# KDA stage: another order of masks, scores and convolutions, and the query's norm taken out of the scores

## The chip, the cores and the metric

One core of a Trainium2 chip runs the whole program in one launch. The metric is device time in microseconds (us), lower is better. Engines: PE does the matmuls, ACT the activations, DVE and POOL the elementwise work, SP starts the transfers.

## What is computed

A network of eight sub-layers runs over 8 sequences of 256 tokens and 256 channels, each as x + layer(layernorm(x)): rwkv7, ffn, rglru, ffn, kda, moe, gqa, moe. The change is in kda, a delta rule with a decay per channel, 16 heads of 128 channels:

```
q, k, v = silu(conv4(x @ Wq)), silu(conv4(x @ Wk)), silu(conv4(x @ Wv))
q, k    = q * rsqrt(sum(q*q) + 1e-6) * 128**-0.5,  k * rsqrt(sum(k*k) + 1e-6)
decay   = exp(-exp(A_log) * softplus(x @ Wfa @ Wfb + dt_bias))
beta    = sigmoid(x @ Wb)
S_t     = decay_t * S_(t-1), then S_t += beta_t * k_t (v_t - k_t S_t);   o_t = q_t S_t
out     = (o * rsqrt(mean(o*o) + 1e-6) * norm_w * sigmoid(x @ Wga @ Wgb)) @ Wo
```

o is linear in q. So a factor on q comes out of o, and the output norm divides it out again, except in its epsilon.

## The kernel before

All activations stay in SBUF. In the KDA stage a *pass* is one head with half of the batch (4 sequences, `UNITS`), 16 heads x 2 halves = 32 passes, written out one after the other without a barrier between them. In a pass each engine runs a fixed list of calls, and its order is the order in the code: `chain_pe`, `chain_act`, `chain_dve`, `chain_pool`. Engines meet through counting semaphores only; an engine that comes to a wait stands, and all that is behind it stands too.

A pass mixes the work of three heads or halves:

- *the chain* of the current one: seven levels l (blocks of 1, 2, 4 ... 64 tokens). POOL scales the query rows and the columns and widens the decays (L1975, L2006, L1983, L1984), DVE scales the key rows (`a_rows`, also L1975), PE makes the scores of a level (`scores`, L2039), DVE masks them into lt and aq_b (`masks`, L2224, L2230). The inverse of a triangular matrix grows level by level: `lt_times_t(l)` on PE (L2064), a copy by ACT (`copy_x(l)`, L2151), `t_times_x(l)` on PE (L2073, L2076), an addition by DVE (`update(l)`, L2245). The last level has forms of its own: `last_scores` (L2051), `last_masks`, `last_x` (L2084), `last_dt` (L2090).
- *the front* of the next one: the decay (low-rank product, clip, exp, log of 1+exp), the convolutions (three taps each on DVE, L1797, over a scaled copy that ACT makes), silu, transposes of the values, and for query and key a square, a sum over channels on PE (`squares`, L1714), logarithm (L1771), exp(-x/2) (`root`, L1785) and a scaling on DVE (`q_row`, `a_row`). `decays` (L1790) makes the decay factors that POOL's first rows wait for. `ahead.project` are the query and key projections (L1681) for the pass after, whose results ACT copies out of PSUM (L1721, L1722).
- *the tail* of the one before: output gate (sigmoid), the state, y, its square sum, `log` (L1934) and `root` (L1939), scaling, the output product `out(k)` (L1911) and the addition to the residual stream on DVE (`residual`, L1968).

Every engine returns to its chain's start when its list ends. PE's list begins with the gate matmuls (L1664, `tail.gate`). PSUM has eight banks: 0 and 1 take the scores and the second head projection, 2 and 3 the products, 4 and 5 the tail, 6 and 7 the front, the first head projection and the second output product `out(1)`. So PE's `out(1)` waits until ACT has copied the first head projection, and the second head projection waits until the last scores are copied:

```python
            pe.wait_ge(n.aq_in_sb, at(n.aq_in_sb, 2))
            ahead.project(1)
            pe.wait_ge(n.ylog, at(n.ylog, 1))
            tail.out(0)
            pe.wait_ge(m.head_read, at(m.head_read, 2))
            tail.out(1)
```

ACT evaluates its functions by tables. Where an activation needs another table than the one that is loaded, the program has an instruction ACT_TABLE_LOAD ahead of it; copies, squares and scalings need none of their own.

Of the kernel before, what the change touches and what calls it, by code (L numbers as in the profile page):

```python
# [17 lines left out]
ALU = mybir.AluOpType  # L18
# [1500 lines left out]
L2_EPS = 1e-6  # L1519
B_LEVELS = LEVELS - 1  # L1520
# [3 lines left out]
def kda(nc, g, a):  # L1524
    with ExitStack() as ctx:
# [6 lines left out]
        with ExitStack() as ctx2:  # L1532
# [28 lines left out]
            with nc.Fori(0, LN_STEPS) as b:  # L1561
                cols = seq_cols(b, LN_COLS // SEQ)
                with nc.Block() as block:
# [16 lines left out]
                    def _(act):  # L1580
# [17 lines left out]
        t1, t2, t3, v_in = (s.sb(x, wide) for x in ("t1", "t2", "t3", "v_in"))  # L1598
        ops = [Names(q=s.sb(f"q{i}", wide), a=s.sb(f"a{i}", wide), f=s.sb(f"f{i}", wide), col=s.sb(f"col{i}", wide),
                     v=s.sb(f"vt{i}", [P, QT, UNITS, P])) for i in range(2)]  # L1600
# [4 lines left out]
        lt6 = s.sb("lt6", [HALF, MATS, HALF])  # L1605
# [4 lines left out]
        bg, e, z = (s.sb(x, [P, UNITS, P]) for x in ("bg", "e", "z"))  # L1610
        d = s.sb("d", [P, QT, UNITS, P])
# [8 lines left out]
                    "dve_step")  # L1620
# [6 lines left out]
            head_ready=2, head_read=4, proj_ready=1, proj_read=2, conv_ready=3, silu_ready=3, sq_ready=2, ss_ready=2,  # L1627
            ss_read=2, rs_ready=2, vt_ready=1, vt_in_sb=1, u_ready=1, log_u=1, inv_ready=1, corr=2, softplus_ready=1,
            decay_ready=1, rows_ready=3, scaled=2 * B_LEVELS, rows_scaled=B_LEVELS, g_step=2 * LEVELS, g_clear=1,
# [47 lines left out]
        def project_pe(w, quad, i, bank, done):  # L1677
            for hf in range(2):
                for k in range(KD):
                    col = K_QKV + (i * KD + k) * P  # L1680
                    last = nc.tensor.matmul(psum(g, bank + hf, BANK), w[:, col:col + P],  # L1681
                                            xn_all[:, k, bass.ds(quad * QUAD + hf * BANK, BANK)], start=k == 0,
                                            stop=k == KD - 1)
            last.then_inc(done, 1)

        def front_pe(pe, o, w, quad):
# [19 lines left out]
            def squares(i):  # L1706
                if i == 0:
                    pe.wait_ge(m.vt_in_sb, at(m.vt_in_sb, 1))
                else:
                    pe.wait_ge(m.ss_read, at(m.ss_read, 1))  # L1710
                pe.wait_ge(m.sq_ready, at(m.sq_ready, i + 1))
                src = (t2, t3)[i]
                for hf in range(2):
                    last = nc.tensor.matmul(psum(g, FRONT + hf, BANK), g.ones_w[:], src[:, 2 * hf:2 * hf + 2],  # L1714
# [5 lines left out]
        def project_act(i, w, bank, done):  # L1720
            nc.scalar.activation(pre[i % 2][:, :, CONV - 1:], two(bank), ACT.Copy).then_inc(done, 1)  # L1721
            nc.scalar.activation(cv[i % 2][:], two(bank), ACT.Identity,  # L1722
                                 scale=w_vec(w, K_CONV + i * CONV + CONV - 1)).then_inc(done, 1)
# [9 lines left out]
        def front_act(act, o, w):  # L1733
# [15 lines left out]
            def silu(i):  # L1749
                if i == 0 and turn.index:  # L1750
                    act.wait_ge(n.final_scaled, at(n.final_scaled, 0))
                act.wait_ge(m.conv_ready, at(m.conv_ready, i + 1))
                nc.scalar.activation((o.q, o.a, v_in)[i][:], cv[i % 2][:], ACT.Silu).then_inc(m.silu_ready, 1)
# [6 lines left out]
            def square(i):  # L1760
                act.wait_ge(m.silu_ready, at(m.silu_ready, i + 1))
                nc.scalar.activation((t2, t3)[i][:], (o.q, o.a)[i][:], ACT.Square).then_inc(m.sq_ready, 1)
# [6 lines left out]
            def log_sum(i):  # L1769
                act.wait_ge(m.ss_ready, at(m.ss_ready, i + 1))  # L1770
                nc.scalar.activation((t2, t3)[i][:], two(FRONT), ACT.Ln, bias=g.eps[:, 2:3]).then_inc(m.ss_read, 1)  # L1771
# [10 lines left out]
            def root(i):  # L1782
                act.wait_ge(m.ss_read, at(m.ss_read, i + 1))
                dst = (t2, t3)[i]
                nc.scalar.activation(dst[:], dst[:], ACT.Exp, scale=-0.5).then_inc(m.rs_ready, 1)  # L1785
# [6 lines left out]
            return Calls(decay=decay, exp_decay=exp_decay, project=project, silu=silu, square=square,  # L1792
# [3 lines left out]
        def tap_dve(step, done, i, j, w):  # L1796
            ins = nc.vector.scalar_tensor_tensor(cv[i % 2][:], pre[i % 2][:, :, j:j + SEQ],  # L1797
                                                 w_vec(w, K_CONV + i * CONV + j), cv[i % 2][:], ALU.mult, ALU.add)
# [5 lines left out]
        def front_dve(dve, step, o, w):  # L1804
# [33 lines left out]
            def a_row():  # L1838
                dve.wait_ge(m.rs_ready, at(m.rs_ready, 2))
# [3 lines left out]
            def column():  # L1843
                dve.wait_ge(m.rows_ready, at(m.rows_ready, 2))
# [4 lines left out]
            return Calls(clip=clip, tap=tap, corr=corr, q_row=q_row, a_row=a_row, column=column)  # L1849

        def tail_pe(pe, o, w, quad):
# [48 lines left out]
            def square_sums():  # L1900
                pe.wait_ge(n.gated, at(n.gated, 2))
                pe.wait_ge(n.ysq, at(n.ysq, 2))
# [15 lines left out]
        def tail_act(act):  # L1918
# [13 lines left out]
            def log():  # L1932
                act.wait_ge(n.yss_ready, at(n.yss_ready, 1))
                nc.scalar.activation(y_sq[:], two(TAIL), ACT.Ln, scale=1.0 / KDA_HEAD, bias=g.eps[:, 2:3]  # L1934
# [8 lines left out]
        def tail_dve(dve, o, w, quad):  # L1943
# [15 lines left out]

            def scale():  # L1960
# [9 lines left out]
            return Calls(inner=inner, right_side=right_side, gate=gate, scale=scale, residual=residual)  # L1970
# [6 lines left out]
        def widen(step, o, l):  # L1977

            h = 1 << l
            blocks = [P, UNITS * SEQ // (2 * h), h]  # L1980
            second_total = halves(o.f[:], h, 1)[:, :, h - 1:h].to_broadcast(blocks)
            first_total = halves(o.f[:], h, 0)[:, :, h - 1:h].to_broadcast(blocks)
            step(nc.gpsimd.tensor_tensor(halves(decay_g[:], h, 0), halves(decay_g[:], h, 0), second_total, ALU.mult))  # L1983
            step(nc.gpsimd.tensor_tensor(halves(o.f[:], h, 1), halves(o.f[:], h, 1), first_total, ALU.mult))  # L1984

        def first_rows(pool, step, o):
# [3 lines left out]
            pool.wait_ge(m.rows_ready, at(m.rows_ready, 2))  # L1990
            for r in range(2):
# [1426 lines left out]
```

## Time and profile before

| | |
|---|---|
| median of 3 runs | 6270.61 us (6264.56 to 6274.58) |
| the profiled execution | 6272.03 us |
| its span | 6270.3 us |
| PE busy, share of the span | 5487.5 us, 88% |
| DVE | 3220.0 us, 51% |
| ACT | 2789.8 us, 44% |
| POOL | 2304.6 us, 37% |
| KDA passes | from about 2171 to 4350 us of the span |

The span is the time on the core between first and last instruction; the execution's time has a few microseconds around it. Busy shares are of the whole program, in which the KDA passes are about a third.

### The profile page before, as it was taken

To read this page: it belongs to the slowest core of one execution; us is meant where nothing else is said; L and a number is where in the kernel's file an instruction comes from. 1 tells how busy PE (TensorE), PEld (TensorE's weight loads), DVE (VectorE), ACT (ScalarE), POOL (GpSimd) and SP (SyncE) were. 2 spreads that over 40 slices of the span, in tenths; PEclk is the share of its full clock that TensorE was granted. 3 is DMA by queue.
4 is the path that set the end of the run, shared out by engine and by line. 5 is a ranking of instruction groups with operands and counts; after the bars stand their busy time and mean duration, and the time that the engine had idled before them with its cause. 6 is when DMAs were issued, how large, how long until landed. Compare 5 with 4: busy or idle time off the path is not lost. (4 is left out here: it accounts for less than half of the span.)

```text
span 6270.3 us, 125078 instructions
## 1 busy us (share of the span) xinstructions
PE 5487.5 (88%) x53008; PEld 3632.2 (58%) x53008; DVE 3220.0 (51%) x4649; ACT 2789.8 (44%) x5107; POOL 2304.6 (37%) x1583
## 2 busy tenths in 40 slices
PE   6888699755999599989989989998999988889999
PEld 5777466543666266666666666665444456664444
DVE  5555444434444376776776677675212166552221
ACT  3233444454444456555655655665211166662111
POOL 4554100001000176777777677675222200002222
PEclk8999799877999799999999999999999988889999
DMA  0000100000000000000000000000211100002111
GB/s 29 3 2 2 33 1 1 16 0 33 1 1 3 22 17 23 18 17 23 18 17 17 24 17 17 23 18 9 107 40 40 34 11 0 0 1 108 39 40 46
DMA packets 60618, 137.02 MB, mean 22 GB/s; under 512 B 11638, under 2 KB 24054, under 8 KB 58842
## 3 DMA queue, kind: packets, MB, share of 16 engines
q1 hardware_dynamic: 60122, 129.79, 6.2%
q8 instruction: 386, 6.32, 0.4%
q14 instruction: 110, 0.90, 0.0%
HBM read 127.26 MB, written 2.50 MB: 21 GB/s over the span
## 5 line engine op out<-in xcount | busy, mean ns | idle before, releaser
L607 PE MATMUL ps<-moe_xn_all,moe_w 128*128 128x512 f32 x1792 | 810.5, 595 | 0.0
L720 DVE TENSOR_TENSOR moe_h<-moe_silu,ps 128x512 f32<-128x512 f32 x224 | 153.9, 687 | 936.2 <-ACT moe_silu L662 929.1
L607 PEld LDWEIGHTS ps<-moe_xn_all,moe_w 128*128 128x128 f32 x1792 | 341.2, 191 | 424.1 <-issue 423.5
L662 ACT ACTIVATE moe_silu<-ps 128x512 f32<-128x512 f32 x224 | 133.8, 597 | 986.5 <-PE ps L607 986.4
L1797 DVE SCALAR_TENSOR_TENSOR kda_cv<-kda_pre,kda_w_front,kda_cv 128x1024 f32<-128x1024 f32 x297 | 554.8, 1885 | 1.3
L563 POOL TENSOR_TENSOR moe_h<-moe_h,moe_cb 128x512 f32<-128x512 f32 x176 | 233.6, 1327 | 696.4 <-DVE moe_h L720 696.4
L1983 POOL TENSOR_TENSOR kda_g<-kda_g,kda_f 128x512 f32<-128x512 f32 x225 | 395.4, 1757 | 205.7 <-DVE kda_rows L1975 197.1
L617 PE MATMUL ps<-moe_h,moe_w 128*128 128x512 f32 x896 | 420.4, 592 | 0.0
L1681 PE MATMUL ps<-kda_xn_all,kda_w_front 128*128 128x512 f32 x808 | 373.6, 606 | 26.0 <-DMA kda_w_front<-in_Kw 23.5
L1975 POOL TENSOR_TENSOR kda_rows<-kda_q,kda_f 128x512 f32<-128x512 f32 x225 | 361.1, 1605 | 16.6 <-POOL kda_f L1984 1.6
L1984 POOL TENSOR_TENSOR kda_f<-kda_f 128x512 f32<-128x512 f32 x225 | 313.9, 1395 | 17.6
L2006 POOL TENSOR_TENSOR kda_cols<-kda_col,kda_g 128x512 f32<-128x512 f32 x192 | 318.6, 1659 | 0.0
L2064 PE MATMUL ps<-kda_t,kda_lt 64*64 64x64 f32 x5120 | 192.3, 227 | 143.4 <-DVE kda_lt L2224 143.4
L2073 PE MATMUL ps<-kda_x_sb,kda_t 64*64 64x32 f32 x5120 | 310.8, 221 | 0.0
L2076 PE MATMUL ps<-kda_t,kda_x_sb 64*64 64x32 f32 x5120 | 307.0, 219 | 0.0
L617 PEld LDWEIGHTS ps<-moe_h,moe_w 128*128 128x128 f32 x896 | 170.2, 190 | 214.3 <-issue 213.3
L2073 PEld LDWEIGHTS ps<-kda_x_sb,kda_t 64*64 64x64 f32 x5120 | 255.6, 135 | 42.2 <-issue 31.8
L2064 PEld LDWEIGHTS ps<-kda_t,kda_lt 64*64 64x64 f32 x5120 | 169.7, 140 | 167.1 <-DVE kda_lt L2224 166.9
L148 POOL TENSOR_TENSOR moe_xn_all<-moe_xn_all,moe_ln_rstd_b 128x1024 f32<-128x1024 f32 x8 | 18.9, 2366 | 665.8 <-DVE moe_ln_rstd_b L240 665.8
L2076 PEld LDWEIGHTS ps<-kda_t,kda_x_sb 64*64 64x64 f32 x5120 | 256.2, 135 | 0.0
L870 ACT ACTIVATE gqa_p<-ps,gqa_nmax 128x256 f32<-128x256 f32 x512 | 236.6, 491 | 36.1 <-DVE gqa_nmax L936 36.1
L1681 PEld LDWEIGHTS ps<-kda_xn_all,kda_w_front 128*128 128x128 f32 x808 | 146.9, 192 | 181.3 <-issue 148.1
(505 smaller groups left out, 12513.3 us busy)
## 6 DMA issues: line engine op xcount, KB each, us to landing
kda_col<-kda_beta SPq DMA_DIRECT2D x34, 512.0 KB, 3.9
moe_w<-in_Mw SPq DMA_DIRECT2D x6, 2816.0 KB, 19.6
moe_cb<-kda_beta SPq DMA_DIRECT2D x64, 256.0 KB, 3.1
kda_w_front<-in_Kw SPq DMA_DIRECT2D x34, 455.0 KB, 4.7
moe_cb<-kda_beta SPq DMA_DIRECT2D x32, 224.0 KB, 2.9
kda_w_out<-in_Kw SPq DMA_DIRECT2D x32, 192.5 KB, 2.4
moe_cb<-kda_beta SPq DMA_DIRECT2D x32, 192.0 KB, 2.8
moe_cb<-kda_beta SPq DMA_DIRECT2D x32, 160.0 KB, 2.7
```

The costliest lines, as they stand in the source:

```text
L607: last = nc.tensor.matmul(ps_gu[u % 2][r], w13[:, k, i, r], n.xn[:, k, cols(c)], start=k == 0, stop=k == KD - 1)
L617: last = nc.tensor.matmul(ps_y[d], w2[:, i, d * P:(d + 1) * P], h[:, u % H_BUFS], start=i == 0, stop=i == M_TILES - 1)
L870: last = nc.scalar.activation(n.p[:, i % 3, j, 0:w], src, ACT.Exp, scale=n.scale, bias=n.nmax[:, i % 2, j:j + 1], accum_out=n.sums[:, q, s ...
L1681: last = nc.tensor.matmul(psum(g, bank + hf, BANK), w[:, col:col + P], xn_all[:, k, bass.ds(quad * QUAD + hf * BANK, BANK)], start=k == 0, ...
L1797: ins = nc.vector.scalar_tensor_tensor(cv[i % 2][:], pre[i % 2][:, :, j:j + SEQ], w_vec(w, K_CONV + i * CONV + j), cv[i % 2][:], ALU.mult, ...
L1975: engine.tensor_tensor(out, halves((o.a, o.q)[r][:], h, 1), halves(o.f[:], h, 1), ALU.mult).then_inc(done, 1)
L1983: step(nc.gpsimd.tensor_tensor(halves(decay_g[:], h, 0), halves(decay_g[:], h, 0), second_total, ALU.mult))
L1984: step(nc.gpsimd.tensor_tensor(halves(o.f[:], h, 1), halves(o.f[:], h, 1), first_total, ALU.mult))
L2006: nc.gpsimd.tensor_tensor(halves(cols_s[l % 2][:], h, 0), halves(cur.col[:], h, 0), halves(decay_g[:], h, 0), ALU.mult).then_inc(n.scaled, 1)
L2064: last = nc.tensor.matmul(ps_x[b, mt], lt[b, l, mt], rhs, start=True, stop=True)
L2073: nc.tensor.matmul(ps_dt[b, mt, 0], t[b, mt, 1], own_half(x_sb[b, mt], h, 0), start=True, stop=True)
L2076: last = nc.tensor.matmul(ps_dt[b, mt, 1], x_sb[b, mt], own_half(t[b, mt, 1], h, 1), start=True, stop=True)
```

## The change

1. The query is no longer scaled. Its square is kept (`q_square`, a new buffer q_sq for each half), and `with_query` on DVE adds 128 x 1e-6 x 128 times that square to the square of y before the sum over channels. The output norm's epsilon becomes 128e-6 x 1e-6. On PE one square sum goes, on ACT one logarithm and one root, on DVE `q_row`.
2. The convolutions are done value, key, query (`PART`). The head projections that are made ahead are now value and key, and the query's silu comes late in the pass.
3. PE's order: scores(l+1) stand behind lt_times_t(l) and ahead of t_times_x(l), the two head projections ahead of last_x and last_dt.
4. DVE: masks stand ahead of clip, taps and updates. POOL: the columns are widened without waiting for the key rows, and the first query rows are scaled behind the widening of the columns.
5. ACT's list in a new order, below.
6. lt6 shares the memory of z; a mask table that nothing reads is no longer loaded.

The core of the diff (taps, signatures and the same edits in the prologue are left out):

```diff
+        PART = (2, 1, 0)
...
             def values():
                 pe.wait_ge(m.proj_read, at(m.proj_read, 2))
-                pe.wait_ge(m.silu_ready, at(m.silu_ready, 3))
+                pe.wait_ge(m.silu_ready, at(m.silu_ready, 1))
...
+            def q_square():
+                act.wait_ge(m.silu_ready, at(m.silu_ready, 3))
+                if turn.index:
+                    act.wait_ge(m.ysum_ready, at(m.ysum_ready, 1))
+                nc.scalar.activation(o.q_sq[:], o.q[:], ACT.Square).then_inc(m.qsq_ready, 1)
...
-            def q_row():
-                dve.wait_ge(m.rs_ready, at(m.rs_ready, 1))
-                nc.vector.scalar_tensor_tensor(o.q[:], o.q[:], float(KDA_HEAD) ** -0.5, t2[:], ALU.mult,
-                                               ALU.mult).then_inc(m.rows_ready, 1)
...
+            def with_query():
+                dve.wait_ge(n.ysq, at(n.ysq, 2))
+                if turn.index:
+                    dve.wait_ge(m.qsq_ready, at(m.qsq_ready, -1))
+                nc.vector.scalar_tensor_tensor(y_sq[:], o.q_sq[:], QUERY_EPS * KDA_HEAD, y_sq[:], ALU.mult,
+                                               ALU.add).then_inc(m.ysum_ready, 1)
...
@@ chain_act, behind tail.gate and f.decay @@
-            f.exp_decay()
             tail.state()
             copy_x(1)
+            f.exp_decay()
+            tail.square(0)
+            copy_x(2)
             f.silu(0)
-            tail.square(0)
             f.project()
-            copy_x(2)
-            f.square(0)
+            copy_x(3)
+            f.values()
+            tail.square(1)
+            copy_x(4)
             f.silu(1)
-            copy_x(3)
-            f.square(1)
+            f.square()
             f.one_plus()
-            tail.square(1)
-            f.silu(2)
-            copy_x(4)
-            act.wait_ge(n.e1_in_sb, at(n.e1_in_sb, 1))
-            f.values()
-            f.log_sum(0)
+            copy_x(5)
             f.log_decay()
-            copy_x(5)
-            f.log_sum(1)
+            f.inverse()
+            f.log_sum()
+            f.root()
             tail.log()
+            f.decays()
...
-            f.inverse()
             copy_x(B_LEVELS, upper)
             tail.root()
-            f.root(0)
-            f.root(1)
-            f.decays()
-            ahead.project(0)
...
             nc.scalar.activation(uf[lower, :, upper], ps_dt6[lower], ACT.Copy).then_inc(n.uf_ready, 1)
+            f.silu(2)
...
+            act.wait_ge(m.silu_ready, at(m.silu_ready, 3))
+            ahead.project(0)
             act.wait_ge(m.corr, at(m.corr, 1))
             act.wait_ge(m.log_u, at(m.log_u, 1))
             ahead.project(1)
+            f.q_square()
@@ chain_dve, behind the first masks @@
+            a_rows(2)
             nc.vector.tensor_tensor(t[:, :, 0], ps_x, ident, ALU.add).then_inc(n.t_ready, 2)
             tail.inner(0)
+            masks(1)
             f.clip()
-            masks(1)
-            a_rows(2)
-            f.tap(0, 1)
-            f.tap(0, 2)
-            f.tap(1, 0)
+            a_rows(3)
+            masks(2)
             update(1)
             tail.gate(0)
...
```

**The order of instructions at three places.** First, ACT in the middle of a pass, from the decay's logarithm (L1775 before, L1782 after) to `decays`. Before:

```order
L1771 ACT_TABLE_LOAD
L1771 ACTIVATE kda_t<-ps,net_eps 128x1024
L1775 ACTIVATE kda_f<-kda_cv 128x1024
L2151 ACTIVATE kda_x_sb<-ps 128x512
L1771 ACTIVATE kda_t<-ps,net_eps 128x1024
L1934 ACTIVATE kda_y_sq<-ps,net_eps 128x1024
L2179 ACTIVATE kda_aq<-ps 64x4x64 x2
L1780 ACT_TABLE_LOAD
L1780 ACTIVATE kda_v_in<-kda_f 128x1024
```

Now:

```order
L1782 ACT_TABLE_LOAD
L1782 ACTIVATE kda_f<-kda_cv 128x1024
L1787 ACT_TABLE_LOAD
L1787 ACTIVATE kda_v_in<-kda_f 128x1024
L1778 ACT_TABLE_LOAD
L1778 ACTIVATE kda_t<-ps,net_eps 128x1024
L1791 ACT_TABLE_LOAD
L1791 ACTIVATE kda_t<-kda_t 128x1024
L1935 ACT_TABLE_LOAD
L1935 ACTIVATE kda_y_sq<-ps,net_eps 128x1024
L1796 ACT_TABLE_LOAD
L1796 ACTIVATE kda_f<-kda_t,kda_rate 128x1024
```

Logarithms (L1782, L1778, L1935) and exponentials (L1787, L1791, L1796) alternate, and each has a load ahead of it. A seventh load stands ahead of the query's silu further on; in all a pass has ten where it had five.

Second, PE near the start of a pass, from the first product to the first t_times_x. Before (lt_times_t(0), the tail's inner product, scores(1), state, lt_times_t(1), y):

```order
L2064 MATMUL ps<-kda_block_ident,kda_lt 64x64 x16
L1868 MATMUL ps<-kda_vt,kda_uf 128x128 x4
L2039 MATMUL ps<-kda_rows,kda_cols 64x64 x16
L1877 MATMUL ps<-kda_d,kda_bg 128x128 x4
L2064 MATMUL ps<-kda_t,kda_lt 64x64 x16
L1889 MATMUL ps<-kda_aq,kda_d 128x128 x4
```

Now:

```order
L2079 MATMUL ps<-kda_block_ident,kda_lt 64x64 x16
L1869 MATMUL ps<-kda_vt,kda_uf 128x128 x4
L2054 MATMUL ps<-kda_rows,kda_cols 64x64 x16
L1878 MATMUL ps<-kda_d,kda_bg 128x128 x4
L2079 MATMUL ps<-kda_t,kda_lt 64x64 x16
L2054 MATMUL ps<-kda_rows,kda_cols 64x64 x16
```

The scores of level 2 follow at once, and y comes behind t_times_x(1).

Third, PE at the end of a pass, from `last_x` or the first head projection to the output product. Before:

```order
L2084 MATMUL ps<-kda_t,kda_lt 64x64 x8
L1681 MATMUL ps<-kda_xn_all,kda_w_front 128x512 x4
L2090 MATMUL ps<-kda_t,kda_x_sb 64x64 x8
L2138 MATMUL ps<-net_ident,kda_cols 128x128 x4
L1681 MATMUL ps<-kda_xn_all,kda_w_front 128x512 x4
L1911 MATMUL ps<-kda_gated,kda_w_out 128x512 x4
```

Now:

```order
L1684 MATMUL ps<-kda_xn_all,kda_w_front 128x512 x4
L2099 MATMUL ps<-kda_t,kda_z 64x64 x8
L1684 MATMUL ps<-kda_xn_all,kda_w_front 128x512 x4
L2105 MATMUL ps<-kda_t,kda_x_sb 64x64 x8
L2156 MATMUL ps<-net_ident,kda_cols 128x128 x4
L1912 MATMUL ps<-kda_gated,kda_w_out 128x512 x4
```

The second projection, which waits for ACT's copies of the last scores, now stands ahead of last_dt.

## Rows read from the trace of the kernel before

**Rows 1.** The page, part 1: busy time, share and instructions of each engine.

```profile
PE 5487.5 (88%) x53008; PEld 3632.2 (58%) x53008; DVE 3220.0 (51%) x4649; ACT 2789.8 (44%) x5107; POOL 2304.6 (37%) x1583
```

**Rows 2.** Timeline of DVE: start, length, operation; the diagonal copy, once a pass.

```profile
2176.43 0.76 DVE L2254 COPY_PREDICATED kda_aq_b<-kda_block_ident,ps 128x512 f32<-128x512 uint32 x1 [0.31 <-PE ps L2100]
...
2378.82 0.74 DVE L2254 COPY_PREDICATED kda_aq_b<-kda_block_ident,ps 128x512 f32<-128x512 uint32 x1
...
2447.89 0.75 DVE L2254 COPY_PREDICATED kda_aq_b<-kda_block_ident,ps 128x512 f32<-128x512 uint32 x1
...
2515.42 0.75 DVE L2254 COPY_PREDICATED kda_aq_b<-kda_block_ident,ps 128x512 f32<-128x512 uint32 x1
...
4291.55 0.74 DVE L2254 COPY_PREDICATED kda_aq_b<-kda_block_ident,ps 128x512 f32<-128x512 uint32 x1
```

**Rows 3.** Window view of the 31 passes: busy time (x instructions) by engine, clock.

```profile
core 0: us, PE busy (x) PEld busy (x) DVE busy (x) ACT busy (x) POOL busy (x), PEclk, DMA share, GB/s
2176.40:4291.60 2115.20, 1913.33 (x28058) 1379.05 (x28052) 1512.50 (x1799) 1269.53 (x1488) 1552.55 (x992) 0.99 0.06 19
```

**Rows 4.** Window view of 5 us in a longer pass.

```profile
2393.00:2398.00 5.00, 3.07 (x66) 2.58 (x65) 4.95 (x7) 2.12 (x4) 2.38 (x3) 0.88 0.00 0
```

**Rows 5.** Timeline of PE over one pass; in brackets idle time before, and for whom.

```profile
2715.48 1.88 PE L1664 MATMUL ps<-kda_ga_all,kda_w_out 128*128 128x512 f32 x4
...
2722.32 1.15 PE L2064 MATMUL ps<-kda_block_ident,kda_lt 64*64 64x64 f32 x32 [1.03 <-DVE kda_lt L2224]
...
2738.64 1.15 PE L2064 MATMUL ps<-kda_t,kda_lt 64*64 64x64 f32 x32 [1.93 <-DVE kda_lt L2224]
...
2756.61 1.98 PE L1714 MATMUL ps<-kda_t,net_ones_w 128*128 128x512 f32 x4
...
2761.28 1.98 PE L1904 MATMUL ps<-kda_y_sq,net_ones_w 128*128 128x512 f32 x4
...
2769.89 1.14 PE L2084 MATMUL ps<-kda_t,kda_lt 64*64 64x64 f32 x16 [0.84 <-DVE kda_lt L2235]
2770.96 3.70 PE L1681 MATMUL ps<-kda_xn_all,kda_w_front 128*128 128x512 f32 x8
2774.59 1.14 PE L2090 MATMUL ps<-kda_t,kda_x_sb 64*64 64x64 f32 x16
...
2779.59 3.60 PE L1911 MATMUL ps<-kda_gated,kda_w_out 128*128 128x512 f32 x8
2783.03 1.88 PE L1664 MATMUL ps<-kda_ga_all,kda_w_out 128*128 128x512 f32 x4
```

**Rows 6.** Groups of ACT in the passes: busy us, mean ns, idle before.

```profile
L2151 ACT ACTIVATE kda_x_sb<-ps 128x512 f32<-128x512 f32 x155 | 92.6, 598 | 258.6 <-PE ps L2064 258.6
...
L1930 ACT ACTIVATE kda_y_sq<-ps 128x512 f32<-128x512 f32 x64 | 37.7, 590 | 86.0 <-PE ps L1889 86.0
...
L1757 ACT ACTIVATE kda_vt<-ps 128x1024 f32<-128x1024 f32 x31 | 31.8, 1025 | 14.7 <-PE ps L1702 14.7
```

**Rows 7.** The same view: a table load, and activations behind loads.

```profile
L1771 ACT ACTIVATE kda_t<-ps,net_eps 128x1024 f32<-128x1024 f32 x62 | 69.1, 1115 | 208.3 <-PE ps L1714 208.3
...
L1771 ACT ACT_TABLE_LOAD x31 | 39.8, 1283 | 0.6
L1780 ACT ACT_TABLE_LOAD x31 | 39.8, 1283 | 0.6
...
L1775 ACT ACTIVATE kda_f<-kda_cv 128x1024 f32<-128x1024 f32 x31 | 32.5, 1047 | 0.0
```

**Rows 8.** Timeline of ACT at the end of that pass.

```profile
2769.54 0.71 ACT L2179 ACTIVATE kda_aq<-ps 64x256 f32<-64x256 f32 x2 [0.22 <-DVE kda_lt L2235]
2770.26 1.28 ACT L1780 ACT_TABLE_LOAD   x1
2771.56 1.06 ACT L1780 ACTIVATE kda_v_in<-kda_f 128x1024 f32<-128x1024 f32 x1
...
2776.12 1.13 ACT L1790 ACTIVATE kda_f<-kda_t,kda_rate 128x1024 f32<-128x1024 f32 x1
2777.27 1.02 ACT L1721 ACTIVATE kda_pre<-ps 128x1024 f32<-128x1024 f32 x1
2778.20 1.11 ACT L1722 ACTIVATE kda_cv<-ps,kda_w_front 128x1024 f32<-128x1024 f32 x1
2779.19 1.28 ACT L2189 ACTIVATE kda_uf<-kda_t 64x512 f32<-64x512 f32 x2
```

**Rows 9.** Timeline of POOL at the end of that pass.

```profile
2778.76 2.47 POOL L1975 TENSOR_TENSOR kda_rows<-kda_a,kda_f 128x512 f32<-128x512 f32 x1 [8.63 <-DVE kda_a L1840]
...
2784.43 1.04 POOL L1984 TENSOR_TENSOR kda_f<-kda_f 128x512 f32<-128x512 f32 x1
```

More of the change, by code:

```diff
@@ L1750, in silu @@
                 if i == 0 and turn.index:
+                    act.wait_ge(m.corr, at(m.corr, 0))
+                if i == 1 and turn.index:
                     act.wait_ge(n.final_scaled, at(n.final_scaled, 0))
                 act.wait_ge(m.conv_ready, at(m.conv_ready, i + 1))
-                nc.scalar.activation((o.q, o.a, v_in)[i][:], cv[i % 2][:], ACT.Silu).then_inc(m.silu_ready, 1)
+                nc.scalar.activation((v_in, o.a, o.q)[i][:], cv[i % 2][:], ACT.Silu).then_inc(m.silu_ready, 1)
             def values():
@@ L1780, in inverse, with root @@
                 nc.scalar.activation(inv_u[:], o.f[:], ACT.Exp, scale=-1.0).then_inc(m.inv_ready, 1)
[L1782 to L1785, printed above, removed]
+            def root():
+                act.wait_ge(m.ss_read, at(m.ss_read, 1))
+                nc.scalar.activation(t3[:], t3[:], ACT.Exp, scale=-0.5).then_inc(m.rs_ready, 1)
             def decays():
@@ L1933, in log @@
                 act.wait_ge(n.yss_ready, at(n.yss_ready, 1))
-                nc.scalar.activation(y_sq[:], two(TAIL), ACT.Ln, scale=1.0 / KDA_HEAD, bias=g.eps[:, 2:3]
+                nc.scalar.activation(y_sq[:], two(TAIL), ACT.Ln, scale=1.0 / KDA_HEAD, bias=g.eps[:, 4:5]
                                      ).then_inc(n.ylog, 1)
@@ L2108, in chain_pe @@
             tail.state()
-            for l in range(1, B_LEVELS):
-                lt_times_t(l)
-                if l == 1:
-                    tail.y_of(0)
-                elif l == 2:
-                    tail.right_side()
-                elif l == 3:
-                    tail.inner(1)
-                elif l == 4:
-                    f.values()
-                else:
-                    tail.square_sums()
-                t_times_x(l)
-                if l == 1:
-                    f.project()
-                elif l == 3:
-                    tail.y_of(1)
-                elif l >= 4:
-                    f.squares(l - 4)
-                if l < B_LEVELS - 1:
-                    scores(l + 1)
-                else:
-                    last_scores()
+            lt_times_t(1)
+            scores(2)
+            t_times_x(1)
+            tail.y_of(0)
+            f.project()
+            lt_times_t(2)
+            scores(3)
+            t_times_x(2)
+            tail.right_side()
+            lt_times_t(3)
+            scores(4)
+            tail.inner(1)
+            t_times_x(3)
+            tail.y_of(1)
+            lt_times_t(4)
+            scores(5)
+            f.values()
+            t_times_x(4)
+            f.squares()
+            lt_times_t(5)
+            last_scores()
+            tail.square_sums()
+            t_times_x(5)
+            pe.wait_ge(m.ss_read, at(m.ss_read, 1))
+            ahead.project(0)
             last_x()
-            pe.wait_ge(m.ss_read, at(m.ss_read, 2))
-            ahead.project(0)
+            pe.wait_ge(n.aq_in_sb, at(n.aq_in_sb, 2))
+            ahead.project(1)
             last_dt()
@@ L2196, in chain_act @@
             ahead.project(1)
-            act.wait_ge(n.sc_done, at(n.sc_done, B_LEVELS))
-            for b in corners:
-                nc.scalar.activation(aq[b, :, b], aq_b[b], ACT.Copy).then_inc(n.aq_in_sb, 1)
+            f.q_square()
         def chain_dve(dve, o, f, tail):
@@ L2294, in chain_dve @@
             f.corr(2)
+            update(5)
+            f.a_row()
+            f.tap(2, 1)
+            f.tap(2, 2)
+            f.column()
             tail.scale()
-            f.q_row()
-            f.a_row()
-            f.column()
             tail.residual(0)
@@ L2389, in _ @@
                 f.project()
-                f.square(0)
+                f.values()
                 f.silu(1)
-                f.square(1)
+                f.square()
                 f.one_plus()
-                f.silu(2)
-                f.values()
-                f.log_sum(0)
-                f.log_decay()
-                f.log_sum(1)
-                f.inverse()
-                f.root(0)
-                f.root(1)
-                f.decays()
+                f.log_decay()
+                f.inverse()
+                f.log_sum()
+                f.root()
+                f.decays()
+                f.silu(2)
+                f.q_square()
                 ahead.project(0)
```

143 lines of the change are left out of this document (72 added, 71 removed).

## The prediction

> **What bounds the kernel now.** The page first: over the whole program TensorE is the busiest engine [rows 1]. The change touches the KDA stage only, so next comes the start of one operation that runs once a pass (DVE's copy of the diagonal) [rows 2]. It stands at 2176.43 us the first time and at 4291.55 us the last, 31 periods later: 68.23 us a pass. Passes come in two lengths: most take 67.54 us (2447.89 to 2515.42) and almost every second one takes 69.07 us (2378.82 to 2447.89). Over these 31 passes PE is busy for 1913 of 2115 us at a granted clock of 0.99 [rows 3]. DVE, POOL and ACT have 28%, 27% and 40% left, so the limit is PE together with the few waits it has.
>
> The longer pass is explained by the window view: in 2393 to 2398 us PE waited and the granted clock fell to 0.88, which means that part of the stretch ran at 1.2 GHz in place of 2.4 [rows 4]. The 1.93 us wait is there in every pass [rows 5]; the fall comes in about every second one and costs 69.07 - 67.54 = 1.53 us.
>
> One pass on PE, from the gate matmuls at 2715.48 us to those of the next pass at 2783.03 us [rows 5], is 67.55 us with eight waits that add up to 6.59 us (1.03 before the first product, 1.93 before the third, 0.84 before the last, and five of 0.20 to 0.77 that don't stand here), nearly all for DVE's masks. So PE has 60.96 us of work a pass. Behind 2770.96 us it never waits.
>
> **What the change does to that.** *The order on PE and DVE.* Scores(l+1) now stand ahead of t_times_x(l), so the mask of a level is made while PE has other work. The orders shown with the change say so. With the durations of one pass laid end to end in the new order I find slack at each of the mask waits: masks(1) is ready about 0.6 us before PE asks for it, the second half of update(2) also about 0.6, all others over 1 us. So the 5.75 us of waits that stand before the end of lt_times_t(5) go. This is the gain.
>
> *Removed on PE.* One square sum, squares(0): four rows of 128x512, 1.91 us from its start to the next operation's at 2756.61 us [rows 5]. PE's work falls to 59.05 us a pass. From gate to the end of lt_times_t(5) both orders do the same operations: before 2761.28 - 2715.48 = 45.80 us, less 5.75 of waits, 40.05 us. The other 19 us come behind.
>
> *A new wait on PE.* ACT now has values() ahead of the copy that t_times_x(4) needs, and PE issues the value transposes just before t_times_x(4). So PE stands for ACT's copy of vt, then square(1), then copy_x(4): 1.03 + 0.59 + 0.60 us by their rows [rows 6], less some 0.1 of overlap, 2.1 us. Lt_times_t(5) ends at 40.05 + 2.1 = **42.15 us** behind the gate.
>
> *Removed and added on ACT and DVE.* ACT loses one logarithm and one root (1.115 us and about 1.0) and keeps the query's square. DVE loses q_row and gains with_query, both a scalar_tensor_tensor of 128x1024: nothing. The mask of 224 KB that isn't loaded at the start is one of five transfers that PE waits for together there, and one more buffer is cleared before the stage; the stage's prologue trades a square sum, a logarithm and a root for three table loads, some microseconds either way; the epilogue gets 1.2 us. I take nothing for all of these, and +-5 us.
>
> *Table loads.* This is the term that decides. ACT's program had five ACT_TABLE_LOAD a pass; now it has ten, because the logarithms and exponentials of the decay, of the key's norm and of the output norm alternate: Ln, Exp, Ln, Exp, Ln, Exp, then Silu for the query, which has moved to the end, ahead of Sigmoid. A load takes 1283 ns in each of its groups [rows 7]. ACT can do nothing meanwhile: the load at 2770.26 us starts as the copies before it end (2769.54 + 0.71) and its activation starts at 2771.56, 1.30 us later [rows 8]. From copy_x(5) to the head copies there was one load; now there are seven.
>
> The Trainium skill ("ScalarE: Activation LUTs", "What ACT_TABLE_LOAD costs") gives 1283 ns for the load and about 1380 ns more for a drain, 2.66 us for each switch. The rows have the first and have no room for the second. By that figure seven switches would cost 9.6 us a pass more than I count, so the trace's 1.29 is used.
>
> *ACT's run, step by step,* with zero where copy_x(5) starts (when lt_times_t(5) ends): copy 0.60, six loads at 1.29, then the 128x1024 activations log_decay 1.05, inverse 1.06, log_sum 1.11, root 1.06, output log 1.11, decays 1.15; the two copies of the last scores 0.71; they end at 15.7 us. PE's second head projection waits for exactly these copies, because it writes the banks that they read; it takes 3.63 (2770.96 to 2774.59) and last_dt 1.08 more, so last_dt ends at 20.4. ACT meanwhile does copy_x(6), the output root, and the four corner copies (2 x 1.28 [rows 8]) and stands at 19.6; it waits to 20.4. Then the uf copy 0.6, load 1.29, silu of the query 1.0, bg 0.5, head copies 0.93 + 1.11 [rows 8]: 25.85 us. PE's out(1) writes the bank that the head copies read, so it starts there, takes half of 3.44 (2779.59 to 2783.03 [rows 5]) and the next gate starts at **27.65 us**. Before, the same stretch was 2783.03 - 2761.28 = 21.75 us.
>
> *The sum:* 42.15 + 27.65 = 69.8 us a pass without a fall of the clock, against 67.54: the front gets 3.65 us shorter and the back 5.9 longer. PE's idle time moves to three stands for ACT: about 1.7 before the first head projection (the key's log_sum ends at 7.5, PE is free at 5.9), 3.1 before the second, 3.4 before out(1), beside the 2.1 at t_times_x(4).
>
> *The clock.* A wait of 1.93 us was followed by a fall in half of the passes [rows 2, 4]. The waits of 3.1 and 3.4 us are longer, so I take a fall behind each of them in each pass. Both lie where it counts: last_dt holds up ACT, and the gate, diagonal and scores behind out(1) start the next pass. 2 x 1.5 = 3.0 us: **72.8 us a pass**. Bounds: none at all, and four falls with the two shorter waits, 6 us.
>
> Against the mean of 68.23: 4.57 x 32 = 146 us. The profiled execution took 6272.0 us (span 6270.3), the median of the runs is 6270.6. Forecast 6270.6 + 146 = **6417 us**.
>
> What covers the rest: POOL's first rows start when decays end, at 14.9 of ACT's run, the query rows wait for the silu at 23.3, and POOL is done with level 0 about 1.6 us before the gate; before, that widen ended 2.4 us behind it (2784.43 + 1.04 [rows 9]). So POOL gets earlier, its idle 8.63 us is room, and if it slipped by more than some 2 us a_rows(2) on DVE would again hold up state. DVE's taps of the key must end 36.9 us behind the gate, where ACT comes to their silu; laid end to end they end at about 34.8.
>
> **Rivals.** *(a) The clock hardly falls.* For it: a fall needs more than one short wait, PE is otherwise full, and part of a fall can lie inside the wait. 69.8 us a pass, at most 70.6: (69.8 - 68.23) x 32 = +50, 6321 us.
> *(b) It falls behind all four waits*, or stays low between the three stands at the end of a pass, where PE is idle for 8 of 22 us. 74.3 to 75.8 us, +194 to +242: 6465 to 6513 us.
> *(c) Faster: the run on ACT isn't longer.* Place: the seven loads between copy_x(5) and the head copies. If Ln and Exp were served by one table, five of these loads would go, 6.45 us; the run ends at 21.2, the pass is 63.3 us, and (63.3 - 68.23) x 32 = -158: 6113 us. It decides from 1.6 us on: as soon as the run is shorter by that, and the clock holds, the pass is below 68.23. Against it: the trace of before has a load ahead of Exp behind Ln in every pass, and the new program lists each load.
> The Trainium skill ("ScalarE: Activation LUTs", "Table sets: the hidden batching unit") says that natural_log_exp_and_others holds both, and that ln then exp takes one load. No row of the KDA stage shows that set in use.
> *(d) A switch costs twice the load* (by the place of the skill on its cost, above): the run grows by seven times about 1.3 us, 79 us a pass, over 6600 us. The rows at 2770.26 and 2771.56 speak against it.
> *(e) It cancels:* the front gains and the back loses alike, within 13 us, for which ACT's run would have to come out 1.6 us shorter than worked out.
>
> **How the numbers follow.** Forecast (two falls, 6385 to 6445) 0.48, (a) 0.20, (b) 0.22, (c) 0.06, (d) 0.01, (e) 0.03. The range reaches from (a) without its last 3 us to the middle of (b): 6318 to 6490. About 0.2% (13 us) is what a measurement of this kernel can tell from no change: faster 0.06, same 0.03, slower 0.91.
>
> **What would show it.** In the trace after: the period of the diagonal copy at 72 to 73 us; ten table loads a pass, 320 in all beside the prologue's; waits of PE's lt_times_t for DVE almost gone, in their place waits for ACT before the head projections, before out(1) and before t_times_x(4); a granted clock over the passes of 0.95 to 0.97 in place of 0.99. Wrong if DVE or POOL is what PE waits for, if the period is below 68, or if the waits on ACT are there and the clock still stays at 0.99, which is (a).

## The result and the profile after

The changed kernel takes 6481.1 us (median of 4 runs, 6470.7 to 6485.8) against 6268.9 us: 1.0336 times the time before, 95% interval 1.0318 to 1.0354. The forecast was 6417 us with a range of 6318 to 6490.

The page's engine totals:

```profile
PE 5602.9 (86%) x52876; PEld 3663.5 (57%) x52876; DVE 3274.6 (51%) x4651; ACT 2945.8 (45%) x5204; POOL 2240.9 (35%) x1583
```

Window view of the 31 periods between the first and the last diagonal copy:

```profile
2170.39:4500.45 2330.06, 2029.80 (x27878) 1414.58 (x27878) 1566.58 (x1798) 1418.65 (x1581) 1492.96 (x994) 0.91 0.06 18
```

Against [rows 3]: 75.16 us a pass in place of 68.23. Over 32 passes that is 222 us, of which 212 are seen in the whole; 6 of the other 10 are the prologue in front of the passes (the first diagonal copy is at 2170.39 us and was at 2176.43). ACT is busier by 4.8 us a pass, PE by 3.8 though it has a square sum less: its clock is 0.91 where it was 0.99.

What PE waited for in these periods: us in all, times, the longest. Before, nearly all of it was DVE's lt.

```profile
PE ps L1912 <- ACT kda_cv L1721: 97.6, 31, 3.2
PE ps L2088 <- ACT kda_x_sb L2167: 64.8, 31, 2.1
PE ps L1684 <- ACT kda_t L1778: 64.3, 31, 2.1
PE ps L1684 <- ACT kda_aq L2194: 59.7, 31, 3.0
PE ps L1878 <- DVE kda_d L1948: 13.2, 11, 1.3
```

299.6 us, 9.7 a pass, where there were 6.5 (201.9 us in all). The mask waits (L2079 for lt) are gone, and in their place PE stands for ACT four times a pass: before out(1), before t_times_x(4), before the first and before the second head projection.

ACT behind copy_x(5), the timeline that answers to [rows 8]:

```profile
2738.57 0.60 ACT L2167 ACTIVATE kda_x_sb<-ps 128x512 f32<-128x512 f32 x1 [3.95 <-PE ps L2079]
2739.18 1.28 ACT L1782 ACT_TABLE_LOAD   x1
2740.47 1.06 ACT L1782 ACTIVATE kda_f<-kda_cv 128x1024 f32<-128x1024 f32 x1
2741.55 1.28 ACT L1787 ACT_TABLE_LOAD   x1
2742.84 1.06 ACT L1787 ACTIVATE kda_v_in<-kda_f 128x1024 f32<-128x1024 f32 x1
2743.92 1.28 ACT L1778 ACT_TABLE_LOAD   x1
2745.21 1.11 ACT L1778 ACTIVATE kda_t<-ps,net_eps 128x1024 f32<-128x1024 f32 x1
...
2753.49 0.63 ACT L2194 ACTIVATE kda_aq<-ps 64x256 f32<-64x256 f32 x2
...
2760.68 0.59 ACT L2204 ACTIVATE kda_uf<-ps 64x512 f32<-64x512 f32 x1 [2.38 <-PE ps L2105]
2761.29 1.28 ACT L1754 ACT_TABLE_LOAD   x1
```

It is one chain without a gap until 2758 us (the rows left out included). PE in the same stretch:

```profile
2733.81 3.63 PE L1713 MATMUL ps<-kda_t,net_ones_w 128*128 128x512 f32 x4
...
2746.38 5.40 PE L1684 MATMUL ps<-kda_xn_all,kda_w_front 128*128 128x512 f32 x8 [2.07 <-ACT kda_t L1778]
2751.71 1.14 PE L2099 MATMUL ps<-kda_t,kda_z 64*64 64x64 f32 x16
2754.17 5.40 PE L1684 MATMUL ps<-kda_xn_all,kda_w_front 128*128 128x512 f32 x8 [1.32 <-ACT kda_aq L2194]
...
2766.09 1.98 PE L1912 MATMUL ps<-kda_gated,kda_w_out 128*128 128x512 f32 x4 [3.15 <-ACT kda_cv L1721]
2767.91 1.88 PE L1667 MATMUL ps<-kda_ga_all,kda_w_out 128*128 128x512 f32 x4
```

Both head projections take 5.40 us where they took 3.70 [rows 5], and the square sum 3.63 where it took 1.98: part of each ran at the lower clock. The groups by shape say where in all passes (busy us, mean ns of one):

```profile
L1684 PE MATMUL ps<-kda_xn_all,kda_w_front 128*128 128x512 f32 x744 | 410.5, 704 | 124.0 <-ACT kda_t L1778 64.3 <-ACT kda_aq L2194 59.7
...
L1912 PE MATMUL ps<-kda_gated,kda_w_out 128*128 128x512 f32 x248 | 156.3, 764 | 97.6 <-ACT kda_cv L1721 97.6
L1713 PE MATMUL ps<-kda_t,net_ones_w 128*128 128x512 f32 x124 | 113.2, 1069 | 0.7
```

Before, the means of these were 601, 592 and 618 ns. Each of the three stands behind one of the waits.

In each pass the trace has three stretches at 1.2 GHz, 13.8 us in all, where the kernel before had 14 in the 31 passes together, 1.5 us a pass. The window view of the three between 3071.81 and 3148.78 us (granted clock 0.50 in each):

```profile
3106.00:3112.83 6.83, 6.83 (x66) 4.23 (x64) 4.79 (x6) 2.00 (x2) 6.13 (x5) 0.50 0.25 79
3129.90:3133.31 3.41, 3.41 (x5) 1.35 (x4) 1.78 (x1) 3.12 (x5) 1.52 (x2) 0.50 0.01 4
3140.14:3146.96 6.82, 6.06 (x7) 2.50 (x8) 2.25 (x3) 4.85 (x5) 5.78 (x5) 0.50 0.11 29
```

One of them stands behind the wait before t_times_x(4) in all 31 passes, the other two behind two of the remaining three waits: 20 times behind the one before the first head projection, 21 before the second, 21 before out(1).

### The profile page after: what moved, and what is told of

Same layout as the page of the kernel before. It is cut to its first block and busy times, and to the rows that moved or that the text cites. A ratio compares the mean times of both kernels' runs of the same rounds, so it can differ in the third digit from the quotient of the medians.

```text
span 6484.0 us, 124940 instructions
## 1 busy us (share of the span) xinstructions
PE 5602.9 (86%) x52876; PEld 3663.5 (57%) x52876; DVE 3274.6 (51%) x4651; ACT 2945.8 (45%) x5204; POOL 2240.9 (35%) x1583
## 5 line engine op out<-in xcount | busy, mean ns | idle before, releaser
L1684 PE MATMUL ps<-kda_xn_all,kda_w_front 128*128 128x512 f32 x808 | 449.8, 710 | 157.5 <-ACT kda_t L1778 70.6
L1803 DVE SCALAR_TENSOR_TENSOR kda_cv<-kda_pre,kda_w_front,kda_cv 128x1024 f32<-128x1024 f32 x297 | 492.5, 1659 | 3.6
L1984 POOL TENSOR_TENSOR kda_rows<-kda_q,kda_f 128x512 f32<-128x512 f32 x225 | 341.7, 1519 | 241.7 <-ACT kda_q L1754 212.2
L2088 PE MATMUL ps<-kda_x_sb,kda_t 64*64 64x32 f32 x5120 | 330.8, 227 | 66.9 <-ACT kda_x_sb L2167 66.9
L1684 PEld LDWEIGHTS ps<-kda_xn_all,kda_w_front 128*128 128x128 f32 x808 | 173.2, 224 | 366.2 <-issue 196.7
L1990 POOL TENSOR_TENSOR kda_g<-kda_g,kda_f 128x512 f32<-128x512 f32 x225 | 339.4, 1509 | 15.1
L2020 POOL TENSOR_TENSOR kda_cols<-kda_col,kda_g 128x512 f32<-128x512 f32 x192 | 336.5, 1752 | 0.0
L2091 PE MATMUL ps<-kda_t,kda_x_sb 64*64 64x32 f32 x5120 | 328.3, 226 | 0.0
L1984 DVE TENSOR_TENSOR kda_rows<-kda_a,kda_f 128x512 f32<-128x512 f32 x192 | 263.9, 1374 | 9.5 <-PEq L84 8.3
L1912 PE MATMUL ps<-kda_gated,kda_w_out 128*128 128x512 f32 x264 | 166.3, 764 | 105.8 <-ACT kda_cv L1721 100.8
```

What stands on the lines that cost most here:

```text
L1984: engine.tensor_tensor(out, halves((o.a, o.q)[r][:], h, 1), halves(o.f[:], h, 1), ALU.mult).then_inc(done, 1)
L2020: nc.gpsimd.tensor_tensor(halves(cols_s[l % 2][:], h, 0), halves(cur.col[:], h, 0), halves(decay_g[:], h, 0), ALU.mult).then_inc(n.scaled, 1)
L2088: nc.tensor.matmul(ps_dt[b, mt, 0], t[b, mt, 1], own_half(x_sb[b, mt], h, 0), start=True, stop=True)
L2091: last = nc.tensor.matmul(ps_dt[b, mt, 1], x_sb[b, mt], own_half(t[b, mt, 1], h, 1), start=True, stop=True)
```

## The experiments

All times are medians, beside runs of the kernel before on the same chip (6268.6 to 6271.1 us); ratios with their 95% interval. Periods are means over 31 passes of the profiled execution.

**One table for Ln and Exp** (from the changed kernel).

```diff
             copy_x(5)
+            nc.scalar.preload_act_table_set(LN_EXP)
             f.log_decay()
```

> The changed kernel with one line more in ACT's list: a load of the table that holds both Ln and Exp, ahead of log_decay. The six loads of the logarithm/exponential chain become one, ten a pass become five, as many as before the change; nothing else moves. Theory A (PE waits for ACT's run, and the loads are what makes it long): the five loads take 6.45 us out of the run, the waits of PE before the first head projection go, before the second shrink under 1.5 us, the period falls from 75.16 to 67 to 69 us and the kernel is near 6260 us (6200 to 6300), level with the one before the change. Rival B (the new order on PE and DVE is slow by itself; ACT is idle 40% of the time and its loads are hidden): at most 1 us a pass comes back, over 6440 us.

6239.8 us, 0.9947 (0.9930 to 0.9963); period 67.33 us, clock 0.96. One line takes 241 us back and makes the changed kernel slightly faster than the one before. The waits left on PE:

```profile
PE ps L1912 <- ACT kda_cv L1721: 82.1, 31, 2.9
PE ps L2088 <- ACT kda_x_sb L2167: 64.8, 31, 2.1
PE ps L1878 <- DVE kda_d L1948: 25.1, 21, 1.3
```

Both waits before head projections are gone. Theory A holds, rival B falls. Rival (c) of the prediction had 63.3 us a pass for this; 5.8 us of waits are left, and 67.33 - 59.05 - 5.77 = 2.5 us is the clock, which (c) took as holding.

The kernel before has this load elsewhere already, in its layer norms (L178), and its trace shows a logarithm (L196) with an exponential (L203) right behind it and no load between:

```profile
1174.70 1.28 ACT L178 ACT_TABLE_LOAD   x1 [4.04 <-PEq L84]
...
1182.81 0.69 ACT L196 ACTIVATE lru_ln_root_b<-ps,net_eps 128x512 f32<-128x512 f32 x1 [0.36 <-PE ps L172]
1183.54 0.72 ACT L203 ACTIVATE lru_ln_root_b<-lru_ln_root_b,net_eps 128x512 f32<-128x512 f32 x1
```

So the remedy could be read from the trace before the change was made.

**The same, with the five loads put back** as loads of the same table, which nothing needs.

```diff
+            nc.scalar.preload_act_table_set(LN_EXP)
             f.inverse()
+            nc.scalar.preload_act_table_set(LN_EXP)
             f.log_sum()
...
```

> The kernel of the first experiment (6240 us, five loads a pass) with five more loads of the same table at the places where the changed kernel has its loads. No activation needs them, and all functions are evaluated by the same table as there. Theory A (the time of the loads themselves is what costs): back to the changed kernel's time, 6465 to 6495 us. Rival G (the joint table is what made the first experiment faster, or the loads of an unchanged table are free): near 6240 us.

6472.3 us, 1.0320 (1.0297 to 1.0343); period 75.16 us, the changed kernel's to the hundredth. So it is the time of the loads, not the table that evaluates the functions; and a load of the table that is already there costs the same 1.28 us:

```profile
2737.93 1.28 ACT L2194 ACT_TABLE_LOAD   x1
2739.22 1.11 ACT L1935 ACTIVATE kda_y_sq<-ps,net_eps 128x1024 f32<-128x1024 f32 x1
2740.35 1.28 ACT L2196 ACT_TABLE_LOAD   x1
2741.65 1.15 ACT L1796 ACTIVATE kda_f<-kda_t,kda_rate 128x1024 f32<-128x1024 f32 x1
```

**The copy for t_times_x(4) first** (from the changed kernel).

```diff
-            f.values()
             tail.square(1)
             copy_x(4)
+            f.values()
```

> The changed kernel with ACT's copy_x(4) ahead of the copy of the values; ten table loads stay. Theory A: the wait before t_times_x(4) (2.1 us in every pass) goes, and with it the fall of the clock behind it (some 1.6 us), while ACT's run behind copy_x(5) keeps its length: 3.7 us a pass, 118 us, 6363 us (6340 to 6420). Rival (ACT's run is the bound by itself, the wait at t_times_x(4) lies beside it): under 0.5 us a pass, 6465 us or more.

6371.5 us, 1.0156 (1.0139 to 1.0173); period 71.69. The wait of 2.1 us is gone, but one of 1.3 us came (PE's key square sum, for ACT's square), and the wait before the second head projection fell by 0.6; in all the waits are 7.8 us a pass where they were 9.7. The pass is shorter by 3.47 us, so the other 1.6 are clock (0.93 in place of 0.91). Theory A holds. The wait of 1.3 us is no cheap one: in all 31 passes a stretch at 1.2 GHz begins within it.

```profile
3059.48 2.04 PE L1713 MATMUL ps<-kda_t,net_ones_w 128*128 128x512 f32 x2 [1.25 <-ACT kda_t L1763]
```

```profile
3059.25:3062.66 3.41, 3.18 (x4) 1.17 (x4) 3.41 (x4) 1.03 (x2) 3.25 (x3) 0.50 0.00 0
```

**Work in the waits** (from the changed kernel): seven matmul instructions a pass whose results nothing reads.

```diff
+            def idle_work(bank, times):
+                for i in range(times):
+                    nc.tensor.matmul(psum(g, bank, BANK), g.ones_w[:], fa_all[:, 0:BANK], start=True, stop=True)
...
             f.values()
+            pe.wait_ge(n.t_ready, at(n.t_ready, 9))
+            idle_work(3, 2)
             t_times_x(4)
...
             t_times_x(5)
+            idle_work(2, 2)
             pe.wait_ge(m.ss_read, at(m.ss_read, 1))
...
             last_x()
+            idle_work(3, 3)
             pe.wait_ge(n.aq_in_sb, at(n.aq_in_sb, 2))
```

> The changed kernel with seven matmul instructions of 128x512 a pass more on PE, that compute nothing used: two before t_times_x(4), two before the first head projection, three before the second, in the places where PE waits for ACT, into banks that are free there. Work is added, none is taken away. Theory A (part of the loss is the clock that falls behind the waits): the granted clock over the passes rises from 0.91 to 0.96 or more, the period falls by 2.5 to 4.5 us, 6340 to 6400 us. Rival (the waits are all, the clock is a by-product of them or costs nothing): no faster than 6460 us, or slower by what of the added 6 us does not fit into the waits.

6352.0 us, 1.0125 (1.0108 to 1.0142); period 71.04. PE has more to do and the kernel is 129 us faster than the changed one. Over the passes:

```profile
2164.39:4366.77 2202.38, 2067.54 (x28326) 1416.76 (x28326) 1590.25 (x1798) 1418.39 (x1581) 1522.92 (x994) 0.98 0.06 19
```

The clock is 0.98. ACT's list is unchanged and so is what PE has to wait for, and at each of the three places PE still stands 0.2 to 0.4 us for ACT, so the added work itself delays nothing. The 4.1 us a pass are what the falls of the clock cost behind three of the four waits: theory A holds. out(1) had no free bank for such work and still waits 3.1 us; behind this wait the clock fell in 23 of 31 passes.

**Only the front's order** (from the kernel before): scores(l+1) ahead of t_times_x(l), masks and key rows ahead of the update, all else as before.

```diff
                 lt_times_t(l)
+                if l < B_LEVELS - 1:
+                    scores(l + 1)
+                else:
+                    last_scores()
...
+            masks(3)
+            a_rows(4)
             update(2)
```

> The kernel before the change with one part of it: scores(l+1) ahead of t_times_x(l) on PE, masks and key rows ahead of the update on DVE. ACT's list, the convolutions, the norm of the query, the end of PE's list and the number of loads (five) stay as before. Theory A (this part is a gain, and the loads ate it): most of the 5.75 us of PE waits for masks go, the clock stays at 1.00, the period falls from 68.2 to 62.5 to 65 us, 6090 to 6170 us. Rival C (DVE and POOL can't deliver the levels earlier, so the waits come back as waits for rows or for the updates): under 1 us a pass, above 6240 us.

6374.9 us, 1.0169 (1.0152 to 1.0186); period 71.68. Theory A missed. Rival C has the time (above 6240 us) and the wait (for an update) right, but not the reason: it isn't DVE's or POOL's speed but the place of the convolution's taps. DVE's timeline in front of update(2), and PE for it:

```profile
2761.86 6.51 DVE L1797 SCALAR_TENSOR_TENSOR kda_cv<-kda_pre,kda_w_front,kda_cv 128x1024 f32<-128x1024 f32 x3
2768.41 0.42 DVE L2224 TENSOR_TENSOR kda_lt<-ps,kda_block_mask 128x256 f32<-128x256 f32 x1
```

```profile
2770.53 1.97 PE L2064 MATMUL ps<-kda_t,kda_lt 64*64 64x64 f32 x32 [4.03 <-DVE kda_t L2245]
```

I had left three taps in a row ahead of masks(3); now the update stands behind that mask, and PE stands 4.0 us for it. The mask waits fell from 6.3 to 2.3 us a pass, but this one came. In all PE waits only 0.6 us a pass more than before (7.1 against 6.5); most of the 3.45 us that the pass got longer is the clock, 0.93 in place of 0.99 (PE is busy 2.7 us more with the same work). The change avoids this wait: it never puts more than two taps ahead of something that PE waits for, which needs another order of ACT's list too. The order of PE is a gain only together with the lists that serve it.

**The old order under one table** (from the first experiment): scores behind t_times_x on PE, masks behind the update on DVE.

```diff
             lt_times_t(1)
-            scores(2)
+            tail.y_of(0)
             t_times_x(1)
-            tail.y_of(0)
             f.project()
+            scores(2)
             lt_times_t(2)
...
```

> The changed kernel with the single table load, and with one part of the change undone: scores(l+1) stand behind t_times_x(l) on PE again, the masks behind the update on DVE. Beside the kernel with the single load and the new order (6240 us) it shows what that order is worth. Theory A (the order takes the mask waits away): 4 to 6 us of waits for masks come back, some of the falls of the clock with them, 6350 to 6450 us. Rival E (the order is worth nothing, the wins are elsewhere): 6225 to 6260 us.

6610.3 us, 1.0545 (1.0527 to 1.0562); period 79.02, 11.7 us more than with the new order. Rival E falls, but the expectation was too small too. 13.2 us of waits a pass; the three largest of seven kinds:

```profile
PE ps L2079 <- DVE kda_lt L2239: 105.5, 124, 1.8
PE ps L2088 <- ACT kda_x_sb L2167: 100.3, 61, 2.1
PE ps L1905 <- DVE kda_y_sq L1965: 66.8, 31, 2.2
```

Only the first are the mask waits, 3.4 us a pass. The rest, 9.8 us, are others, for ACT and for DVE's other work; that they come of old and new lists that don't fit each other is my reading, no run took them apart. So 11.7 us is no clean price of the order.

**Only the fold of the query's norm** (from the kernel before).

```diff
-                elif l >= 4:
-                    f.squares(l - 4)
+                elif l == 4:
+                    f.squares()
...
             tail.gate(1)
+            tail.with_query()
...
-            f.q_row()
             f.a_row()
```

> The kernel before the change with the query's norm folded into the output norm alone (one square sum less on PE, one logarithm and one root less on ACT, with_query for q_row on DVE, the query's square at the end of ACT's list); orders, convolutions and table loads as before, five a pass. Theory A (PE's list is the bound there, so its 1.91 us come out of each pass): 61 us, 6209 us (6195 to 6225). Rival F (PE then stands 1.9 us for the last masks or for ACT instead): 6255 us or more.

6153.8 us, 0.9818 (0.9801 to 0.9834); most periods 64.50, the mean 64.83: 3.40 us a pass where 1.91 was expected. 1.91 is the square sum. 0.93 is waits (172.9 us in all against 201.9): ACT has two activations less ahead of `decays`, so POOL's first rows and with them DVE's first come earlier, and the 1.03 us wait at the first product [rows 5] is gone. Of the rest, 0.55, some 0.36 is the clock, which falls in every sixth pass (66.6 us) in place of every second: 68.23 - 67.54 = 0.69 us a pass before, 64.83 - 64.50 = 0.33 now. The last 0.19 stays open. The time is below theory A's range (6195 to 6225), rival F falls. This part of the change was right by itself.

**All of ACT's waits taken away** (from the changed kernel).

```diff
+            nc.scalar.preload_act_table_set(LN_EXP)
             f.log_decay()
...
             tail.root()
+            f.silu(2)
+            act.wait_ge(m.silu_ready, at(m.silu_ready, 3))
+            ahead.project(0)
             act.wait_ge(n.t_ready, at(n.t_ready, 2 * B_LEVELS + 1))
...
-            f.squares()
             lt_times_t(5)
             last_scores()
+            f.squares()
...
-            a_rows(2)
             dve.wait_ge(n.x_ready, at(n.x_ready, 1))
             nc.vector.tensor_tensor(t[:, :, 0], ps_x, ident, ALU.add).then_inc(n.t_ready, 2)
             tail.inner(0)
+            a_rows(2)
             masks(1)
```

(and copy_x(4) ahead of values, as above)

> The changed kernel with its waits for ACT taken away one by one: the single table load of the first experiment; copy_x(4) ahead of the values' copy; the key's square sum on PE behind last_scores in place of ahead of lt_times_t(5); the query's silu and the first head copies on ACT ahead of the copies into uf and aq, so that out(1) needn't wait; a_rows(2) on DVE behind the tail's first copy in place of ahead of it. Theory A: PE has 59.05 us of work a pass, and with 2 to 4 us of waits left and few falls of the clock the period is 62.5 to 64.5 us, 6080 to 6150 us. Rival D (with ACT's waits gone DVE or POOL is the next bound at once, as they hold a chain of their own through the seven levels): 65.5 us or more, 6190 us or more, and PE's waits name DVE or POOL.

6111.8 us, 0.9751 (0.9735 to 0.9768); period 63.33. PE's waits are down to 3.1 us a pass:

```profile
PE ps L1912 <- DVE kda_gated L1971: 75.4, 31, 2.4
PE ps L2079 <- DVE kda_t L2260: 19.2, 31, 0.6
```

Theory A holds. The largest wait is for DVE, as rival D has it, but for one operation that stood too far back in its list. So it was moved:

```diff
-            copy_x(B_LEVELS, upper)
             tail.root()
+            copy_x(B_LEVELS, upper)
...
             f.tap(2, 1)
+            tail.scale()
             f.tap(2, 2)
             f.column()
-            tail.scale()
```

> The kernel of the fifth experiment (6112 us, period 63.3 us) with tail.root ahead of copy_x(6) on ACT and tail.scale ahead of the last tap on DVE. There PE stood 2.4 us a pass for scale ahead of out(0), and nearly nowhere else. Theory: this wait goes, with what the clock lost behind it, the period falls to 60 to 61.5 us, 6005 to 6055 us. Rival (the last tap and with it the query's silu and the head copies come 1.2 us later, so that out(1) waits for ACT instead): 6085 us or more.

6062.6 us, 0.9670 (0.9650 to 0.9689), the fastest here; period 61.69 in all passes, clock 1.00. It lies between the two expectations: the 2.4 us wait went, and 2.2 us for the head copies came:

```profile
PE ps L1912 <- ACT kda_cv L1721: 40.6, 31, 1.3
PE ps L2054 <- ACT kda_cv L1721: 28.6, 31, 0.9
PE ps L2079 <- DVE kda_t L2260: 19.2, 31, 0.6
```

Nearly as much waiting as before the move, yet 1.64 us a pass faster: spread over 1.3, 0.9 and 0.6 us it doesn't bring the clock down, in one piece of 2.4 us it did (0.97).

## Why the prediction was right

It was right in sign, mechanism and range, by these steps:

- *PE is the limit, and the mask waits go*: shown. No wait for lt is left in the changed kernel.
- *Seven loads in one run of ACT*: shown by the first experiment and by the five loads put back. Worked out were 15.7 us from copy_x(5) to the end of the copies of the last scores; measured are 2753.49 + 0.63 - 2738.57 = 15.55. (The terms of the prediction add up to 15.59, not 15.7, and its 25.85 + 3.44 / 2 is 27.57, not 27.65.)
- *The waits on ACT*: 1.7, 3.1, 3.4 and 2.1 us were forecast, 10.3 in all without falls of the clock; the four measured means are 2.1, 1.9, 3.1 and 2.1, 9.2 in all. The second is 3.0 us in passes in which the first projection ran at full clock and 1.3 us in the others, because the slow projection ahead of it fills part of it. The forecast's own 69.8 us leave 10.75 us of waits beside 59.05 of work; 0.45 of them stand in no term.
- *A wait that the sum didn't have*: state on PE for DVE (0.43 us a pass, at most 1.3). I named its condition, a_rows(2) on DVE, and thought that it wouldn't be met. The durations that I laid end to end on DVE were too short. a_rows(2) took 1.75 us, where I had used 0.7; such an operation takes 0.68 us when POOL is idle and 1.75 when POOL works all the while. The first tap, for which I had used 1.9, took 2.54 us in one pass of three, and these are the passes with the wait; in the others it took 1.28.
- *The table load costs 1.29 us, with no drain behind it*: the trace after agrees, since each activation starts 0.01 us behind its load. The Trainium skill ("ScalarE: Activation LUTs", "What ACT_TABLE_LOAD costs") gives 2.66 us for a switch; the estimate from it, rival (d), is above 6600 us, and the measurement decides against it. The Trainium skill's other rule ("ScalarE: Activation LUTs", "Table sets: the hidden batching unit"), that one table holds both Ln and Exp, is what the first experiment uses: it holds when the program asks for that table by name. In the KDA passes of the change nobody asked, and the trace has a load wherever a logarithm and an exponential alternate.

**The term that was mis-sized is the clock's:** "a fall behind each of them in each pass. [...] 2 x 1.5 = 3.0 us". With PE's work of 59.05 and waits of 9.66, the period of 75.16 leaves 6.45 us, twice as much and what four falls of 1.53 would cost. They are three stretches at 1.2 GHz a pass, some of them twice as long as those before. I counted only waits longer than the 1.93 us of the kernel before and left the two of 2.1 us to rival (b). The trace has it otherwise: one wait of 2.1 us, the one before t_times_x(4), has a fall behind it in every pass, the wait of 3.1 us before out(1) only in 21 of 31. The length of a wait alone didn't decide. Rival (b)'s 6465 to 6513 us is what was measured. The rows of before gave a warning: 1.93 us gave a fall in every second pass, so 2.1 us deserved at least a half.

The front and prologue terms that I took at nothing came out at about -10 us in the whole: the changed prologue is shorter by 6 us.

That the time lies inside the range, 9 us below its upper bound, is partly luck. The pass without falls came out at 59.05 + 9.66 = 68.7 us where the sum had 69.8, 35 us in 32 passes, and the ends gave another 10. With the clock's term alone off, the time would have been about 6526 us by this estimate, outside.

## What to carry to other kernels

Count table loads in the order of the program, not functions: logarithms and exponentials that alternate cost a load each unless the joint table is named, and an engine that is idle 40% of the time can still hold the one that is the limit if the loads lie in one run between two hand-overs. Price a wait of the matmul engine with what its clock loses behind it, but don't expect one price. Here four waits of 2 to 3 us in a pass lost 6.45 us; one of 1.93 us among shorter ones lost 0.69 us a pass in the kernel before and 0.33 with the fold alone; waits of 1.3, 0.9 and 0.6 us in the fastest kernel lost nothing, while one of 1.3 us ahead of waits of 2.1, 1.3 and 3.1 had a fall behind it in every pass. When one engine's list is reordered, look in the lists that serve it for the longest piece of other work ahead of each hand-over.

## What was not expected of the hardware

Loading the table that is already active takes the same 1.28 us as a switch. And matmuls that compute nothing, put where PE stood idle, made the kernel 129 us faster, by a granted clock of 0.98 in place of 0.91. Where exactly in a pass the clock falls varies in a fixed rhythm (periods of 76.97, 74.27 and 74.04 us in turn); each has three stretches at 1.2 GHz, of 17.1, 10.2 and 13.7 us together, and why they differ is left open.
